# Score and value products of a windowed attention on 64-row tiles, one head each, interleaved in two passes

## The chip, the cores and the metric

One core of a Trainium2 chip. The metric is the device time of one execution in microseconds (us), the median of several runs of the same program. Profiles are of one execution each.

## What is computed

Four sequences of 512 tokens by 128 channels. A cross attention on a short context comes first (it takes the first 50 us and the change touches only where it keeps its operands). Then come six layers, each a windowed attention and a feed-forward block, all in float32. The attention of a layer:

```python
qkv = x @ Wqkv                          # 16 heads of 64
q = l2norm(q) * qs ;  k = l2norm(k) * ksc
q = q*cos*scale + rotate_half(q)*sin*scale      # k with 1/scale
# windows of 32 queries; each sees its own 32 keys and the 32 before
sim  = einsum('bhwie,bhwje->bhwij', bq, bk2) * 8
attn = softmax(where(mask, -max, sim), -1)
out  = einsum('bhwij,bhwje->bhwie', attn, bv2)
x = out @ Wo + x
```

The feed-forward block is a layer norm over channels, `x @ W1`, a gated gelu, `@ W2`, and a residual.

## The kernel before

**Units and slots.** A unit is 128 tokens of one sequence by 8 of the 16 heads of one layer. Eight units make a group (one sequence in one layer, 4 blocks of tokens times 2 halves of the heads), 24 groups make 192 units. Every engine has its own instruction stream, written as a loop over slots n (line 541 for PE, and one each for ACT, DVE, POOL and SP); s is n % 8. In slot n an engine works on several units at different stages; the stages are set by hand, by the order of calls in each loop. Nothing is scheduled by a compiler. Semaphores join the engines.

**A unit's way.** PE makes q and k (`queries_keys`, line 376) and v (`values`, 389). ACT squares q and k (618), DVE sums the squares per head (`sum_squares`, 824), ACT makes a seed of the inverse root, DVE refines it in three short operations (`newton`, 837, 840, 842) and scales k and q into SBUF (`scale_k` 850, `scale_q` 858, which signals `qn_done`). POOL rotates both in six instructions (1053, 1060, 1096 for k, then 1053, 1060, 1089 for q). PE transposes k (410) and q (399), ACT copies them to `kB` (654) and `qT` (645). PE adds the scores (423) to a mask that ACT has put into the bank `sc_bank` (664). DVE takes maxima (865) and subtracts them into `pr` (873), ACT makes the exponentials (671), PE transposes them (`transpose_p`, 436), and the value product (`attend`, 448) multiplies them with the windows of v in `vw`. DVE scales the result into `o` (`scale_o`, 898), PE transposes `o` (461), ACT copies it to `oT` (690), and once per half group PE projects it (472). Slots s = 2, 3, 6 and 7 hold extra long products of PE: the two projections (s = 2, 6), four products of the feed-forward block (s = 3) and its second matrix (s = 7); s = 0, 1, 4, 5 hold one shorter product each. DVE's longest extra work lies in s = 3: two additions to x (907, 908), `rstd_newton` (938, 940), and, after `scale_o`, `layer_norm` (947), for which the four products on PE wait.

**Order in a slot on DVE.** `sum_p`, `newton`, `scale_k`, `scale_q` (of unit n-2), `maxima`, `invert_sum`, `less_maxima` (of n-4), work of the feed-forward block, `sum_squares`, `clamp_squares`, and nearly last `scale_o` (of n-5). PE's first product of a slot waits for `qn_done` of unit n-2:

```python
pe.wait_ge(qn_done, past(u - 1))
```

**Scores and values on PE.** Two heads lie on the 128 partitions of qT. `kB` holds k of both heads in 128 columns with zeros where the other head's rows are (so it is copied by two ACT instructions of 64 partitions), and `vw` is laid out likewise. One product has a contraction of 128, 32 columns of weights (a window of queries) and 128 moving columns (two heads of 64 keys). The array is cut into four column tiles of 32, one per window; 4 pairs of heads times 4 windows make 16 products a unit. Each product in float32 shows as two passes in the profile (x32 a unit).

**PSUM.** q and k have two double banks. One bank is for scores. All else goes round three banks, `RING[i % RINGS]`: each use takes the next turn i, and PE waits until the use three turns earlier has been read (`ring_read`).

**v windows.** ACT copies v from PSUM to `vs` (627). SP then copies its windows to `vw` by DMA (`v_copies`, issues at 1181, 1184, 1187), 8 or 10 transfers a unit, as soon as the value product of two units before is finished. ACT waits before `vs` is used again, six units later.

## Time and profile before

| | us |
|---|---|
| median of 3 runs | 1827.32 |
| lowest, highest run | 1821.96, 1829.11 |
| the profiled execution | 1824.23 |
| its span, first to last instruction | 1822.2 |

| engine | busy us | share of the span |
|---|---|---|
| PE | 1750.3 | 96% |
| DVE | 1619.0 | 89% |
| POOL | 1500.4 | 82% |
| ACT | 1327.5 | 73% |

The profile follows one execution. PE is the matmul part of TensorE, PEld its weight loads, DVE is VectorE, ACT is ScalarE, POOL is GpSimd and SP issues DMAs. In a timeline a row is a run of like instructions: start, length, engine, line of the kernel, output and inputs, and how many; in brackets the engine's idle time before it and what ended that. PE's products overlap, so the length of a row reaches into the next; what a stage costs is the distance from its start to the start of the next. The granted clock of TensorE is at its upper level (1.00) in the whole middle part.

### The profile page before, as it was taken

What the parts mean: (1) busy time and instruction counts of PE and PEld (TensorE: products, weight loads), DVE (VectorE), ACT (ScalarE), POOL (GpSimd) and SP (SyncE); (2) the same over time, 40 slices, a digit from 0 to 9 for tenths busy, and PEclk for the clock granted to TensorE, in tenths of its full rate; (3) what the DMA queues carried; (4) which work ended last, traced back from release to release, by engine and by line L of the source; (5) the groups of instructions that cost most, each with busy time, mean ns of one, the idle gap of its engine ahead of it and who ended that gap; (6) DMA issues with size and microseconds to landing.
All of it is one profiled execution on the core that took longest, in us unless ns stands there. A gap on an engine that the chain in (4) does not pass through costs nothing.

```text
span 1822.2 us, 48666 instructions
## 1 busy us (share of the span) xinstructions
PE 1750.3 (96%) x18122; PEld 1116.2 (61%) x18122; DVE 1619.0 (89%) x2782; ACT 1327.5 (73%) x2362; POOL 1500.4 (82%) x1204
## 2 busy tenths in 40 slices
PE   7699999999999999999999999999999999999986
PEld 6356666666666666666666666666666666666663
DVE  7799998999999989989999999899999998988874
ACT  3577877877778778778777777787776877877763
POOL 4799888888888888988888888888888888888860
PEclk9999999999999999999999999999999999999998
DMA  4132222222222222322223222222222222222221
GB/s 114 28 87 67 68 71 57 60 73 76 71 63 69 63 66 71 76 65 68 63 56 81 72 70 72 54 63 73 75 72 62 68 58 58 59 71 56 56 64 29
DMA packets 155273, 120.59 MB, mean 66 GB/s; under 512 B 42607, under 2 KB 151457, under 8 KB 154913
## 3 DMA queue, kind: packets, MB, share of 16 engines
q1 hardware_dynamic: 155041, 117.48, 25.1%
q8 instruction: 147, 2.41, 0.6%
q14 instruction: 85, 0.70, 0.1%
HBM read 18.79 MB, written 1.05 MB: 11 GB/s over the span
## 4 chain that ended last, share of the span: by engine, by line
PE 77%; DVE 13%; POOL 5%; issue 3%; SPq 1%; ACT 1%; DMA 1%; DVEq 0%; POOLq 0%; ACTq 0%
PE qk_bank L376 17%; PE ring_bank L448 10%; PE ring_bank L472 9%; PE ring_bank L389 8%; PE sc_bank L423 7%; PE ring_bank L516 6%; PE ring_bank L436 4%; PE ring_bank L399 3%; PE ring_bank L527 3%; PE ring_bank L461 3%; PE ring_bank L410 3%; DVE rn L842 2%; DVE step L837 2%; DVE o L898 2%; DVE qkn L858 2%
## 5 line engine op out<-in xcount | busy, mean ns | idle before, releaser
L1053 POOL TENSOR_TENSOR turned<-qkn,tables 128x512 f32<-128x512 f32 x384 | 489.3, 1274 | 209.8 <-DVE qkn L850 201.5
L1060 POOL TENSOR_TENSOR turned<-qkn,tables 128x512 f32<-128x512 f32 x384 | 496.7, 1294 | 0.0
L376 PE MATMUL qk_bank<-wqkv,xT 128*128 128x512 f32 x768 | 366.5, 600 | 18.8 <-DVE qkn L858 18.6
L1089 POOL TENSOR_TENSOR turned<-turned 128x512 f32<-128x512 f32 x192 | 255.0, 1328 | 15.1
L1096 POOL TENSOR_TENSOR turned<-turned 128x512 f32<-128x512 f32 x192 | 245.1, 1277 | 15.1
L448 PEld LDWEIGHTS ring_bank<-vw,pT 128*32 128x32 f32 x6144 | 156.6, 110 | 143.8 <-issue 143.7
L654 ACT ACTIVATE kB<-ring_bank 64x512 f32<-64x512 f32 x384 | 225.3, 587 | 23.5 <-PE ring_bank L410 21.2
L824 DVE TENSOR_REDUCE ss<-sq 128x16 f32<-128x1024 f32 x192 | 232.0, 1208 | 6.8 <-ACT sq L618 6.8
L627 ACT ACTIVATE vs<-ring_bank 128x512 f32<-128x512 f32 x192 | 114.7, 598 | 163.1 <-PE ring_bank L389 153.4
L898 DVE TENSOR_TENSOR o<-ring_bank,rr 128x512 f32<-128x512 f32 x192 | 132.1, 688 | 104.2 <-PE ring_bank L448 101.3
L389 PE MATMUL ring_bank<-wqkv,xT 128*128 128x512 f32 x384 | 216.1, 645 | 1.6 <-DVE x L978 1.6
L664 ACT ACTIVATE sc_bank<-mask_f 128x512 f32<-128x512 f32 x192 | 114.5, 596 | 136.0 <-DVE pr L873 135.6
L448 PE MATMUL ring_bank<-vw,pT 128*32 128x128 f32 x6144 | 208.4, 276 | 0.1
L423 PE MATMUL sc_bank<-kB,qT 128*32 128x128 f32 x6144 | 207.5, 276 | 0.3
L376 PEld LDWEIGHTS qk_bank<-wqkv,xT 128*128 128x128 f32 x768 | 131.2, 191 | 121.7 <-issue 93.4
L618 ACT ACTIVATE sq<-qk_bank 128x1024 f32<-128x1024 f32 x192 | 198.0, 1031 | 0.0
L423 PEld LDWEIGHTS sc_bank<-kB,qT 128*32 128x32 f32 x6144 | 156.0, 109 | 34.7 <-issue 34.7
L472 PE MATMUL ring_bank<-oT,wo 128*128 128x256 f32 x768 | 173.8, 379 | 0.0
L461 PEld LDWEIGHTS ring_bank<-ident,o 128*128 128x128 f32 x768 | 95.5, 141 | 102.1 <-issue 83.9
L472 PEld LDWEIGHTS ring_bank<-oT,wo 128*128 128x128 f32 x768 | 142.2, 190 | 18.1 <-DVE uT L956 0.8
L516 PE MATMUL ring_bank<-xnT,w 128*128 128x512 f32 x288 | 143.3, 609 | 8.5 <-DVE xnT L947 7.3
L850 DVE TENSOR_TENSOR qkn<-qk_bank,rn 128x512 f32<-128x512 f32 x192 | 132.9, 692 | 20.7 <-DVE rn L842 0.9
(169 smaller groups left out, 3129.3 us busy)
## 6 DMA issues: line engine op xcount, KB each, us to landing
vw<-vs SPq DMA_DIRECT2D x1152, 64.0 KB, 2.1
vw<-vs SPq DMA_DIRECT2D x672, 32.0 KB, 1.9
wqkv<-in_L_ffn_Wqkv_dram SPq DMA_DIRECT2D x20, 384.0 KB, 3.5
wo<-in_L_ffn_Wo_dram SPq DMA_DIRECT2D x20, 128.0 KB, 3.3
w<-in_L_ffn_W_dram SPq DMA_DIRECT2D x6, 341.0 KB, 3.4
wqkv<-in_L_ffn_Wqkv_dram SPq DMA_DIRECT2D x1, 1536.0 KB, 9.5
x<-in_x_dram SPq DMA_DIRECT2D x2, 512.0 KB, 4.7
out_dram<-x SPq DMA_DIRECT2D x4, 256.0 KB, 2.3
```

The lines of the kernel that those rows point to most:

```text
L376: mm = pe.matmul(QK[u % 2][:, i * UW:(i + 1) * UW], tok, wqkv[:, layer % 2, cut:cut + UW], start=True, stop=True)
L389: pe.matmul(RING[i % RINGS][:, :], xT[:, b, t * P:(t + 1) * P], wqkv[:, layer % 2, cut:cut + UW], start=True, stop=True).then_inc(ring_mad ...
L423: mm = pe.matmul(heads(SC_BANK[WIN * w:WIN * (w + 1), k * P:(k + 1) * P]), qT[:, u % 2, k, WIN * w:WIN * (w + 1)], kB[:, HP * half + k, :, ...
L448: mm = pe.matmul(heads(RING[i % RINGS][WIN * w:WIN * (w + 1), k * P:(k + 1) * P]), pT[:, u % 2, k, WIN * w:WIN * (w + 1)], vw[:, u % 2, w, ...
L472: mm = pe.matmul(RING[i % RINGS][:, 0:HALF], wo[:, layer % 2, k, :], oT[:, k, HALF * h:HALF * (h + 1)], start=(k == 0), stop=(k == KO - 1))
L516: pe.matmul(RING[i % RINGS][:, :], w1[:, DFF * j + k * P:DFF * j + (k + 1) * P], xnT[:, :], start=True, stop=True).then_inc(ring_made[i % ...
L654: ev = act.activation(kB[64 * h:64 * h + 64, HP * half:HP * half + HP, h, WIN + P * t:WIN + P * t + P], RING[i % RINGS][64 * h:64 * h + 64 ...
L824: dve.tensor_reduce(ss[:, :], heads(sq[:, :]), AX.X, ALU.add).then_inc(ss_done, 1)
L1053: return pool.tensor_tensor(heads(turned[:, u % 2, 2 * i, :]), heads(qkn[:, u % 2, i * UW:(i + 1) * UW]), table.unsqueeze(1).to_broadcast( ...
L1060: return pool.tensor_tensor(halves(turned[:, u % 2, 2 * i + 1, :]), halves(qkn[:, u % 2, i * UW:(i + 1) * UW])[:, :, ::-1, :], table.rearr ...
L1089: pool.tensor_tensor(q, q, turned[:, u % 2, 1, :], ALU.add).then_inc(q_summed, 1)
L1096: pool.tensor_tensor(k, k, turned[:, u % 2, 3, :], ALU.add).then_inc(k_summed, 1)
```

## The change

Each head gets products of its own. A score or value product is now 64 rows (one head), 32 columns of weights and 64 moving columns, and its tile position has a row part too: head 0 of a pair is on rows 0 to 63, head 1 on rows 64 to 127. There are 32 score and 32 value products a unit. `kB` becomes `kT` without the zero blocks (one ACT copy of 128 partitions in place of two), `vw` loses them too, and the memset of `vw` moves from the end of the cross attention to the start.

The products run in two passes, each with both kinds interleaved. Pass one is the score products of head 0 and the value products of head 1; pass two is the rest. Within a pass, the two row halves so write different banks. `scores_values` (pass one) stands behind `values`, `scores_values_rest` (pass two) behind `transpose_o`. A new semaphore, `first_half`, holds pass two until pass one is complete.

```diff
-            def scores(u):
...
+            def score(u, k, w, h):
                 g, layer, b, t, half = place(u)
-                pe.wait_ge(mask_done, u + 1)
-                pe.wait_ge(*evicted("q", u))
+                rows, c0 = slice(DH * h, DH * (h + 1)), P * t + WIN * w
+                return pe.matmul(SC_BANK[WIN * w:WIN * (w + 1), (2 * k + h) * DH:(2 * k + h + 1) * DH],
+                                 qT[rows, u % 2, k, WIN * w:WIN * (w + 1)], kT[rows, HP * half + k, c0:c0 + 2 * WIN],
+                                 start=False, stop=True, tile_position=(DH * h, WIN * w), skip_group_check=True)
+
+            def value(u, k, w, h):
+                rows, bank = slice(DH * h, DH * (h + 1)), RING[turns["pv", u] % RINGS]
+                return pe.matmul(bank[WIN * w:WIN * (w + 1), (2 * k + h) * DH:(2 * k + h + 1) * DH],
+                                 pT[rows, u % 2, k, WIN * w:WIN * (w + 1)], vw[rows, u % 2, w, k * DH:(k + 1) * DH],
+                                 start=True, stop=True, tile_position=(DH * h, WIN * w), skip_group_check=True)
+
+            def scores_values(us, uv):
+                s_on, v_on = 0 <= us < UNITS, 0 <= uv < UNITS
+                if s_on:
+                    pe.wait_ge(mask_done, us + 1)
+                    pe.wait_ge(*evicted("q", us))
+                if v_on:
+                    i = turn("pv", uv)
+                    pe.wait_ge(vw_dma[uv % 2], vw_count(uv))
+                    pe.wait_ge(ring_read[i % RINGS], i // RINGS)
+                    pe.wait_ge(*evicted("p", uv))
                 for k in range(HP):
                     for w in range(NW):
...
+                        if s_on:
+                            last_score = score(us, k, w, 0)
+                        if v_on:
+                            last_value = value(uv, k, w, 1)
...
+            def scores_values_rest(us, uv):
+                s_on, v_on = 0 <= us < UNITS, 0 <= uv < UNITS
+                pe.wait_ge(first_half, past(min(us + 1, UNITS)) + past(min(uv + 1, UNITS)))
...
+                            last_score = score(us, k, w, 1)
+                        if v_on:
+                            last_value = value(uv, k, w, 0)
+                if s_on:
+                    last_score.then_inc(score_mm, 1)
+                if v_on:
+                    last_value.then_inc(ring_made[turns["pv", uv] % RINGS], 1)
...
             for n in range(SLOTS):
                 g, s = n // UPG, n % UPG
                 queries_keys(n)
-                attend(n - 5)
                 values(n)
+                scores_values(n - 3, n - 5)
                 transpose_o(n - 6)
-                scores(n - 3)
+                scores_values_rest(n - 3, n - 5)
                 transpose_p(n - 4)
...
-                for h in range(2):
-                    ev = act.activation(kB[64 * h:64 * h + 64, HP * half:HP * half + HP, h, WIN + P * t:WIN + P * t + P],
-                                        RING[i % RINGS][64 * h:64 * h + 64, :].rearrange("p (k q) -> p k q", q=P), ACT.Copy)
-                ev.then_inc(ring_read[i % RINGS], 1)
+                act.activation(kT[:, HP * half:HP * half + HP, WIN + P * t:WIN + P * t + P],
+                               RING[i % RINGS][:, :].rearrange("p (k q) -> p k q", q=P),
+                               ACT.Copy).then_inc(ring_read[i % RINGS], 1)
...
                 if s == 1:
+                    finish(g - 3)
                     centre(g - 2)
...
-                if s == 1:
-                    finish(g - 3)
...
+            pool.memset(vw[:, :, :, :], 0.0).then_inc(vw_zero, 1)
...
-            pool.wait_ge(b_xT, B)
-            pool.memset(free, 0.0).then_inc(vw_zero, 1)
```

How PE's stream moves, first from the start of a slot with s = 1, before the change (376 q and k, 448 value product, 389 v, 461 transposes of o, 423 scores, 436 transposes of p; the names behind "waits" are semaphores, and `ring_readN` is the reading of bank N):

```order
L376 MATMUL qk_bank<-wqkv,xT 128x512 [waits qn_done]
L376 MATMUL qk_bank<-wqkv,xT 128x512
L448 MATMUL ring_bank<-vw,pT 32x128 [waits ring_read1,ring_read2,vw_dma0]
L448 MATMUL ring_bank<-vw,pT 32x128 x15
L389 MATMUL ring_bank<-wqkv,xT 128x512 [waits ring_read0]
L461 MATMUL ring_bank<-ident,o 128x128 [waits ring_read1]
L461 MATMUL ring_bank<-ident,o 128x128 x3
L423 MATMUL sc_bank<-kB,qT 32x128 [waits ring_read1,mask_done]
L423 MATMUL sc_bank<-kB,qT 32x128 x15
L436 MATMUL ring_bank<-ident,pr 128x128 [waits exp_done,ring_read2]
```

And with the change the same slot's start (373 q and k, 386 v, 414 a score product, 420 a value product; the last two then alternate 16 times):

```order
L373 MATMUL qk_bank<-wqkv,xT 128x512 [waits qn_done]
L373 MATMUL qk_bank<-wqkv,xT 128x512
L386 MATMUL ring_bank<-wqkv,xT 128x512 [waits ring_read2]
L414 MATMUL sc_bank<-kT,qT 32x64 [waits ring_read0,vw_dma0,ring_read1,mask_done]
L420 MATMUL ring_bank<-vw,pT 32x64
```

The value product has gone from second to third place, and its first half shares the first wait with the scores: for the mask, for qT and pT (both `ring_read1`), for its own bank (`ring_read0`), and for the windows of v. In the same slot, the end of pass one, the transposes of o (476) and the start of pass two:

```order
L414 MATMUL sc_bank<-kT,qT 32x64
L420 MATMUL ring_bank<-vw,pT 32x64
L476 MATMUL ring_bank<-ident,o 128x128 [waits ring_read2,ring_read1]
L476 MATMUL ring_bank<-ident,o 128x128 x3
L414 MATMUL sc_bank<-kT,qT 32x64 [waits first_half]
L420 MATMUL ring_bank<-vw,pT 32x64
```

The last value product, which DVE's `scale_o` waits for, lies behind all of these. Last, the same stream from the scores to the transposes of k, before:

```order
L423 MATMUL sc_bank<-kB,qT 32x128 [waits ring_read1,mask_done]
L423 MATMUL sc_bank<-kB,qT 32x128 x15
L436 MATMUL ring_bank<-ident,pr 128x128 [waits exp_done,ring_read2]
L436 MATMUL ring_bank<-ident,pr 128x128 x3
L410 MATMUL ring_bank<-ident,turned 128x128 [waits k_summed,ring_read0]
```

and with the change (466 transposes of p, 407 transposes of k):

```order
L414 MATMUL sc_bank<-kT,qT 32x64
L420 MATMUL ring_bank<-vw,pT 32x64
L466 MATMUL ring_bank<-ident,pr 128x128 [waits exp_done,ring_read2]
L466 MATMUL ring_bank<-ident,pr 128x128 x3
L407 MATMUL ring_bank<-ident,turned 128x128 [waits k_summed,ring_read0]
```

The transposes of k take bank 0 in both. Before, the use of bank 0 three turns earlier was v, which ACT reads; now it is the value product, which DVE reads in `scale_o`.

## Rows read from the trace of the kernel before

**Rows 1.** The page's part 4: shares of the span in the chain.

```profile
PE 77%; DVE 13%; POOL 5%; issue 3%; SPq 1%; ACT 1%; DMA 1%; DVEq 0%; POOLq 0%; ACTq 0%
```

**Rows 2.** Stretches: us, busy (x) of PE, PEld, DVE, ACT, POOL; clock, DMA, GB/s.

```profile
62.00:110.00 48.00, 37.33 (x398) 21.55 (x397) 45.22 (x64) 32.00 (x61) 47.06 (x39) 0.96 0.17 43
...
900.00:972.00 72.00, 70.80 (x757) 44.83 (x750) 66.24 (x111) 54.51 (x98) 61.88 (x50) 1.00 0.26 65
```

**Rows 3.** Timeline of PE: start us, us busy; first q/k product of slots.

```profile
906.03 1.98 PE L376 MATMUL qk_bank<-wqkv,xT 128*128 128x512 f32 x4 [0.43 <-DVE qkn L858]
...
926.74 1.88 PE L376 MATMUL qk_bank<-wqkv,xT 128*128 128x512 f32 x4
...
934.29 1.88 PE L376 MATMUL qk_bank<-wqkv,xT 128*128 128x512 f32 x4
...
942.69 1.98 PE L376 MATMUL qk_bank<-wqkv,xT 128*128 128x512 f32 x4 [0.68 <-DVE qkn L858]
...
952.94 1.88 PE L376 MATMUL qk_bank<-wqkv,xT 128*128 128x512 f32 x4
...
977.86 1.55 PE L376 MATMUL qk_bank<-wqkv,xT 128*128 128x512 f32 x3 [0.36 <-DVE qkn L858]
```

**Rows 4.** Timeline of PE: stages of the slot from 942.69.

```profile
944.61 1.08 PE L448 MATMUL ring_bank<-vw,pT 128*32 128x128 f32 x32
...
945.62 1.13 PE L389 MATMUL ring_bank<-wqkv,xT 128*128 128x512 f32 x2
...
946.58 0.60 PE L461 MATMUL ring_bank<-ident,o 128*128 128x128 f32 x4
...
947.11 1.08 PE L423 MATMUL sc_bank<-kB,qT 128*32 128x128 f32 x32
...
948.61 0.60 PE L410 MATMUL ring_bank<-ident,turned 128*128 128x128 f32 x4
```

**Rows 5.** Timeline of DVE, from `scale_o` to the scaling of q.

```profile
929.80 0.69 DVE L898 TENSOR_TENSOR o<-ring_bank,rr 128x512 f32<-128x512 f32 x1 [0.65 <-PE ring_bank L448]
...
931.00 0.17 DVE L837 SCALAR_TENSOR_TENSOR step<-seed 128x16 f32<-128x16 f32 x1
...
931.20 1.14 DVE L840 TENSOR_TENSOR step<-step,ssm 128x16 f32<-128x16 f32 x1
...
932.38 0.17 DVE L842 SCALAR_TENSOR_TENSOR rn<-step,seed 128x16 f32<-128x16 f32 x1
...
933.26 0.68 DVE L858 TENSOR_TENSOR qkn<-qk_bank,rn 128x512 f32<-128x512 f32 x1
```

**Rows 6.** Timeline of POOL: last of a unit; first and last of the next.

```profile
931.01 1.30 POOL L1089 TENSOR_TENSOR turned<-turned 128x512 f32<-128x512 f32 x1
...
933.49 1.28 POOL L1053 TENSOR_TENSOR turned<-qkn,tables 128x512 f32<-128x512 f32 x1 [1.18 <-DVE qkn L850]
...
939.91 1.30 POOL L1089 TENSOR_TENSOR turned<-turned 128x512 f32<-128x512 f32 x1
```

**Rows 7.** The chain in order of time: start us, us, what.

```profile
916.44 1.72 PE qk_bank L376 x4
```

**Rows 8.** Timeline of ACT: mask, then (third in order) qT.

```profile
944.06 0.60 ACT L664 ACTIVATE sc_bank<-mask_f 128x512 f32<-128x512 f32 x1 [2.01 <-DVE pr L873]
...
945.34 0.60 ACT L645 ACTIVATE qT<-ring_bank 128x512 f32<-128x512 f32 x1
```

**Rows 9.** Timeline of DVE: `scale_o` of s=2, of s=3, and the normalisation.

```profile
909.36 0.68 DVE L898 TENSOR_TENSOR o<-ring_bank,rr 128x512 f32<-128x512 f32 x1
...
920.55 0.69 DVE L898 TENSOR_TENSOR o<-ring_bank,rr 128x512 f32<-128x512 f32 x1
...
921.16 1.05 DVE L947 SCALAR_TENSOR_TENSOR xnT<-dT,cols,rstd 128x512 f32<-128x512 f32 x1
```

**Rows 10.** Timeline of SP: three issues of the v copies.

```profile
910.35 1.87 SPq L1181 DMA_DIRECT2D vw<-vs  x3
```

**Rows 11.** The page's part 6: size and us to landing.

```profile
vw<-vs SPq DMA_DIRECT2D x1152, 64.0 KB, 2.1
```

More of the change, by code:

```diff
@@ L126, in build @@
         rr = sb("rr", [P, 2, HU])
-        free = vw[:, :, :, :, :].rearrange("p k w h n -> p (k w h n)")
-        def take(start, groups, width):
-            return free[:, start:start + groups * width].rearrange("p (a c) -> p a c", c=width)
-        wx_in, wxT = take(0, 4, C), take(512, 4, C)
-        ctx_sb, vx = take(1024, B, C)[0:CTX], take(1536, B, C)[0:CTX]
-        ctxT, kxT = take(2048, B, CTX), take(2560, B, CTX)
+        chunk = lambda c, groups, width: kT[:, c, WIN:WIN + groups * width].rearrange("p (a c) -> p a c", c=width)
+        wx_in, wxT = chunk(0, 4, C), chunk(1, 4, C)
+        ctx_sb, vx = chunk(2, B, C)[0:CTX], chunk(3, B, C)[0:CTX]
+        ctxT, kxT = chunk(4, B, CTX), chunk(5, B, CTX)
         bcol = sb("bcol", [P, 2])
@@ L234, in build @@
         mask_done = sem("mask_done")
+        first_half = sem("first_half")
         score_mm = sem("score_mm")
@@ L436, in transpose_p @@
                     mm = pe.transpose(RING[i % RINGS][:, k * P:(k + 1) * P], pr[:, u % 2, k * P:(k + 1) * P], ident[:, :])
-                mm.then_inc(ring_made[i % RINGS], 1)
-            def attend(u):
-                if not 0 <= u < UNITS:
-                    return
-                i = turn("pv", u)
-                pe.wait_ge(vw_dma[u % 2], vw_count(u))
-                pe.wait_ge(ring_read[i % RINGS], i // RINGS)
-                pe.wait_ge(*evicted("p", u))
-                for k in range(HP):
-                    for w in range(NW):
-                        mm = pe.matmul(heads(RING[i % RINGS][WIN * w:WIN * (w + 1), k * P:(k + 1) * P]),
-                                       pT[:, u % 2, k, WIN * w:WIN * (w + 1)],
-                                       vw[:, u % 2, w, :, k * DH:(k + 1) * DH], start=True, stop=True,
-                                       tile_position=(0, WIN * w))
                 mm.then_inc(ring_made[i % RINGS], 1)
```

34 lines of the change are left out of this document (16 added, 18 removed).

## The prediction

> **What bounds the kernel now.** I read the chain of waits first: three quarters of the span lie on PE and a seventh on DVE, nothing on DMA [rows 1]. The stretch view says how full the engines are: of 72 us in the middle PE is busy for 70.8, DVE for 66.2, POOL for 61.9 [rows 2]. So PE is the bound, but DVE stands only 5 us of 72 behind it. Then the timeline, slot by slot. A **slot** is one turn of the loop over n (one unit of attention, from one first q/k product to the next); eight slots, s = 0 to 7, are one group. The eight slots from 906.03 to 977.86 take 71.8 us [rows 3]: s=2 and s=3 together 20.7, s=4 7.55, s=5 8.4, s=6 10.25, s=7, 0 and 1 together 24.9. Slots 2, 3, 6 and 7 carry the long extra products of PE; the others are the **light** ones, and there PE waits for others.
>
> The loop that decides in a light slot runs through PE and DVE and closes once a slot. PE(n) needs qn_done of unit n-2, which is the last thing that DVE makes in its head of slot n. That stands behind scale_o of the slot before, and scale_o waits for the value product of the slot before. So slot length >= a + b, where **a** is the time from PE's first q/k product to the start of scale_o, and **b** from scale_o's start to PE's next q/k product.
>
> b: scale_o starts at 929.80; the scaling of q that follows it ends at 933.94, and PE starts 0.06 behind such an end (as 942.69 does where it waited): 4.20 us. In it L840 takes 1.14 us where its neighbour L842 takes 0.17; it ends at 932.34, when the POOL instruction of 931.01 ends (932.31) [rows 5, 6]. So a short DVE operation on SBUF is held until the running POOL instruction is over. Without it b is 4.20 - 0.97 = 3.23, say 3.2. The Trainium skill (SBUF — State Buffer, "SBUF: two separate sides") calls the pair of ports of VectorE and GpSimd an exclusive lock; by that rule the trace agrees.
>
> a now: PE 942.69 to 944.61, and the value product ends at 945.69 [rows 3, 4]: 3.0 us, 3.1 with the hand-over. Then a + b is 6.3 to 7.3. DVE has its own work for the first 3.3 us: at 909.36 scale_o starts that long after PE's 906.03 without having waited [rows 3, 9]. At 929.80 it waited 0.65 us [rows 5], so the path is nearly taut already.
>
> **What the change does to PE.** Full array: four passes of 512 columns take 1.72 us [rows 7], so 128 columns take 0.1075. The present score or value stage is 32 passes of 128 columns, 3.44 us one at a time; it takes 1.01 us from its start to the next (944.61 to 945.62) [rows 4]: 0.86 with four tiles side by side, and 0.15 for going in. Each new stage is half of both products: 32 products, 64 passes of 64 columns, again 3.44 us one at a time. With eight tiles (two of rows, four of columns) it is 0.43 + 0.15 = 0.58. Bounds: below that only with more than eight tiles, which there are not; with four at a time still 1.01; and if what spaces the passes is their issue, not the array, the present mean of 1.01/32 = 31.6 ns holds for each of 64: 2.02. I take 0.58, because weight loads and products of one stage now come 32 to a microsecond and the stage comes out at a whole quarter of the array's time, which an issue limit would hit by accident only. Saved on PE: 2 x 0.43 = 0.86 us a slot, 7 us of 72. The number of changes between the two array modes stays four.
>
> **What it does to the loop.** The value product was second in the slot; now it ends with the second pass, behind v, both passes and the transposes of o. And its first pass is queued behind the waits of the scores. Going through a slot in which PE waited at the start:
> - q/k to the next stage is 1.92 now, 1.72 of passes and 0.2 for the first weight load and the change of mode, half each (I split it so; the sum does not hang on it). So v starts at 1.82, takes 0.86, and with the change of mode pass one could issue at 2.78 [rows 4, 7].
> - Its score half waits for qT. ACT copies qT third, behind the mask and the exponentials, and those wait for DVE's pr: the copy ends at 945.34 + 0.60 = 945.94, 3.25 us after PE's start [rows 3, 8]. Now scores start at +4.4 (947.11) and this is hidden; then it is not. Pass one starts at 3.3.
> - 0.58 for it, transposes of o 0.53 (946.58 to 947.11) plus the 0.10 that v takes now, coming after a packed stage (0.96 instead of 0.86), 0.58 for pass two: 5.07. The last product ends 0.07 behind the next start and the hand-over is 0.1 [rows 4]. **a = 5.3**. Where PE did not wait at the start qT is early, and a = 1.72 + 0.96 + 0.58 + 0.63 + 0.58 + 0.17 = 4.7.
>
> DVE's own work still lasts 3.3 us, so it then stands idle for 2 us in each light slot, in order, with the sum, the three Newton steps and both scalings queued behind scale_o, and POOL and PE behind those.
>
> b then: POOL's six instructions of a unit start at 933.49, half a us before the 934.00 at which PE could, and take 7.72 (to 941.21) [rows 5, 6]. So POOL runs until +7.2. The first Newton step comes 1.2 after scale_o, at +6.5, and is held until POOL is through (its last instruction runs from +5.9). From the end of POOL's last instruction to its next first are then 1.18 (printed as its idle time) plus one more short step, 0.2. **Light slot: 7.72 + 1.18 + 0.2 = 9.1 us**, for any a from 4.7 to 6.0; beyond, a + 3.2.
>
> The eight slots:
> - s=2 and 3: scale_o of s=2 at 5.3; from there to the scale_o of s=3 DVE works 11.2 us (its other work of both slots lies there, so it does not shrink) (909.36 to 920.55), to the end of the normalisation 1.66 (922.21), and from there PE, whose gate products need it, takes 4.5 to the next slot (926.74) [rows 3, 9]: 22.7 instead of 20.7.
> - s=4: DVE ahead, a = 4.7, b between 3.2 and 4.2: 8.4 (7.55 now). s=5: 9.1 (8.4).
> - s=6: passes end at 5.1, then the transposes of p; those of k wait for scale_o to read their bank (order rows above), 5.3 + 0.69 + 0.06 = 6.05, and from there to the next slot as now 948.61 to 952.94, 4.3 [rows 3, 4]: 10.4 (10.25). What PE saves is eaten by qT and that bank.
> - s=7: PE bound, no wait at the start: transposes of k at 4.7 + 0.75 = 5.45, those of k and q 0.44 each (four passes of 128 columns), the second matrix six passes of 0.43: 8.9. s=0 and 1: 9.1 each. 27.1 together (24.9).
>
> Sum 77.7 against 71.8: +5.9, times 22 groups = +130. In the opening, without feed-forward work, POOL is the bound (busy 47.1 of 48 us [rows 2]) at 7.7 a slot; the 11 slots from the first value product (n = 5) to the end of group 1 go to 9.1: +15. In the tail the products thin out: 0.
>
> **At nothing:** the one copy of kT in place of two saves ACT 0.6 us, hidden by ACT's 2.01 us wait for DVE [rows 8]. The v copies on SP start as now when the value product of two units before is done; nine or ten issues of 0.62 and 2.1 to land [rows 10, 11] make 8.4, well inside two slots of 9.1; ACT's copy of v, which waits for them, comes at about +4.6 and its bank is wanted at +5.1. Cover gone, each 0.5 late would cost up to 0.5 a slot. Smaller memsets at the start lie before POOL's first work. `finish` moves over nothing but DVE's last group.
>
> The profiled execution took 1824.2 us (span 1822.2), 3 below the median of the runs. 1824 + 130 + 15 = 1969; I say **1970**.
>
> **Rivals.**
> 1. *Row tiles do not run side by side* (the change does not do what it says): passes 1.01. a = 6.2, light 9.4; 23.6 + 9.3 + 9.4 + 11.3 + 9.8 + 18.8 = 82.2, +10.4 x 22 + 18: 2070. Nothing in the trace has two row tiles, so nothing speaks against it.
> 2. *Issue bound*: passes 2.02, a = 8.2, light 11.4; 25.6 + 11.3 + 11.4 + 13.3 + 11.8 + 22.8 = 96.2, +24.4 x 22 + 42: 2400. For it: the number of passes doubles, 31.6 ns is all that the rows show.
> 3. *Faster*: PE's saving decides and the late value product does not, because DVE's work still fills the time before scale_o. The group then falls to what DVE is busy, 66.2 [rows 2]: -5.6 x 22: 1700. For it: PE is the bound and is relieved by more than that. It decides if a stays below about 3.5, where DVE's own work covers it; against it: PE's passes alone add up to 4.7.
> 4. *No change*: the loop is there, but qT is in time (a = 4.7) and POOL holds nothing (b = 3.22): light 7.9, 22.1 + 7.9 + 7.9 + 9.6 + 8.8 + 15.8 = 72.1, +0.3 x 22: 1831. Against it: POOL is at work for 62 of 72 us [rows 2], so a free moment of 0.6 us must fall just right.
>
> The Trainium skill (TensorE: Matmul & The Clock Gate, Part 1, "Wait — 56ns, not 53.3ns?") says that starts of matmuls never come closer than about 25 ns however few the columns. By it a pass would be 64 x 25 ns = 1.6 us, an estimate from the page, and the kernel about 2260. No row here parts that from rival 2; the 31.6 ns lie above it, so the trace neither bears it out nor contradicts it.
>
> **How the numbers follow.** Forecast 0.68, rival 1 0.13, rival 2 0.06, rival 3 0.07, rival 4 0.06. The range, 1850 to 2085, holds the forecast with a light slot from 8.3 to 9.5 and rival 1; outside are the other three, 0.19. Faster by over 0.5% (what a measurement of this kernel can tell; its runs lie within 0.4%): rival 3 and a tail, 0.08. Same: most of rival 4, 0.05. Slower: 0.87.
>
> **What would show it.** Right: PE's two pass stages near 0.6 us each; DVE's idle time before scale_o, waiting for the value product, at some 2 us in nearly each slot (now 0.65 at 929.80); light slots at 9 us; PE busy near 85%; POOL waiting for the k scaling in almost each slot, and the first Newton step ending with POOL's last instruction. Wrong: stages of 1.0 or 2.0 (rivals 1, 2), or scale_o not waiting (3), or Newton steps of 0.2 in light slots (4).

## The result and the profile after

| | before | after |
|---|---|---|
| median | 1826.4 us (1822.0 to 1829.1, 4 runs) | 2075.4 us (2066.2 to 2086.0, 4 runs) |
| ratio, 95% interval | | 1.137 (1.131 to 1.143) |
| span of the profiled execution | 1822.2 us | 2083.9 us |

The kernel became 13.7% slower, 105 us more than forecast and 10 us inside the upper end of the range. The page of the kernel after, its parts 1, 3 and 4, and the queue's line of before:

```profile
span 2083.9 us, 73056 instructions
...
PE 1789.4 (86%) x30410; PEld 1117.8 (54%) x30410; DVE 1464.9 (70%) x2782; ACT 1196.3 (57%) x2170; POOL 1490.3 (72%) x1203
...
q8 instruction: 243, 3.98, 0.8%
...
PE 56%; DVE 28%; issue 10%; SPq 3%; POOL 1%; DMA 1%; DVEq 1%; ACT 1%; POOLq 0%; ACTq 0%
```

```profile
q8 instruction: 147, 2.41, 0.6%
```

DVE's part of the chain rose from 13% to 28% [rows 1]. "Issue", time in which an engine waited for nothing that the profile shows, rose from 3% to 10%; the order alone does that too, since experiment 1 below, which has no stop, shows 9%. The groups of instructions of the kernel after (line, engine, operation, shapes, count | busy us, mean ns | idle time before, and what ended it):

```profile
L1064 POOL TENSOR_TENSOR turned<-qkn,tables 128x512 f32<-128x512 f32 x384 | 487.9, 1270 | 470.8 <-DVE qkn L864 470.8
...
L912 DVE TENSOR_TENSOR o<-ring_bank,rr 128x512 f32<-128x512 f32 x192 | 132.8, 691 | 509.8 <-PE ring_bank L420 509.4
L373 PE MATMUL qk_bank<-wqkv,xT 128*128 128x512 f32 x768 | 382.9, 622 | 62.6 <-DVE qkn L872 62.6
...
L414 PE MATMUL sc_bank<-kT,qT 64*32 64x64 f32 x12288 | 332.9, 224 | 74.2 <-issue 58.0
L420 PE MATMUL ring_bank<-vw,pT 64*32 64x64 f32 x12288 | 337.8, 225 | 26.5 <-issue 26.5
```

and `scale_o` of the kernel before:

```profile
L898 DVE TENSOR_TENSOR o<-ring_bank,rr 128x512 f32<-128x512 f32 x192 | 132.1, 688 | 104.2 <-PE ring_bank L448 101.3 <-ACT qT L645 0.5
```

DVE's wait for the value product grew from 101 to 509 us, 2.7 us a slot: this is the late value product of the forecast. The 84 us of "issue" in the two lines of the passes nobody had forecast; the same two groups of before, L423 and L448, have 0.3 and 0.1 us of idle time.

A **light slot** after (993.29 to 1002.37, s = 5), DVE and then POOL, and PE's next q/k product:

```profile
998.83 0.69 DVE L912 TENSOR_TENSOR o<-ring_bank,rr 128x512 f32<-128x512 f32 x1 [2.17 <-PE ring_bank L420]
999.44 0.68 DVE L894 TENSOR_REDUCE rs<-pr 128x8 f32<-128x512 f32 x1
1000.03 0.47 DVE L851 SCALAR_TENSOR_TENSOR step<-seed 128x16 f32<-128x16 f32 x1
1000.53 0.18 DVE L854 TENSOR_TENSOR step<-step,ssm 128x16 f32<-128x16 f32 x1
1000.75 0.17 DVE L856 SCALAR_TENSOR_TENSOR rn<-step,seed 128x16 f32<-128x16 f32 x1
1001.02 0.69 DVE L864 TENSOR_TENSOR qkn<-qk_bank,rn 128x512 f32<-128x512 f32 x1
1001.63 0.68 DVE L872 TENSOR_TENSOR qkn<-qk_bank,rn 128x512 f32<-128x512 f32 x1
```
```profile
999.19 1.27 POOL L1100 TENSOR_TENSOR turned<-turned 128x512 f32<-128x512 f32 x1
1001.86 1.26 POOL L1064 TENSOR_TENSOR turned<-qkn,tables 128x512 f32<-128x512 f32 x1 [1.39 <-DVE qkn L864]
```
```profile
1002.37 1.98 PE L373 MATMUL qk_bank<-wqkv,xT 128*128 128x512 f32 x4 [0.84 <-DVE qkn L872]
```

`scale_o` waits 2.17 us (2 forecast) and starts 5.54 us into the slot (a, 5.3 forecast). The first Newton step takes 0.47 instead of 0.17: it ends at 1000.50, when POOL's instruction of 999.19 is over (1000.46). The slot is 9.08 us (9.1 forecast).

**The passes.** A pass here is one half of the products: 32 products, which show as 64 matmul records, and 64 weight loads. The timeline of PE in the slot from 985.00 (the first two starts of pass one, the transposes of o, the start of pass two and the transposes of p):

```profile
987.67 0.24 PE L414 MATMUL sc_bank<-kT,qT 64*32 64x64 f32 x1
987.68 0.24 PE L420 MATMUL ring_bank<-vw,pT 64*32 64x64 f32 x1
...
988.46 0.66 PE L476 MATMUL ring_bank<-ident,o 128*128 128x128 f32 x4
989.04 0.24 PE L414 MATMUL sc_bank<-kT,qT 64*32 64x64 f32 x1
...
989.83 0.66 PE L466 MATMUL ring_bank<-ident,pr 128*128 128x128 f32 x4
```

A pass takes 0.79 us from its start to the next stage (987.67 to 988.46), not 0.58. **A stop in pass two** of the slot from 1002.37:

```profile
1007.43 0.22 PE L414 MATMUL sc_bank<-kT,qT 64*32 64x64 f32 x1
1009.29 0.21 PE L420 MATMUL ring_bank<-vw,pT 64*32 64x64 f32 x1 [1.65 <-issue]
```

The pass stands still for 1.86 us, six of its 64 matmul records short of its end; DVE's `scale_o`, and all behind it, come that much later. There are 41 such gaps of over 0.9 us between the starts of neighbouring products of a pass, 72.2 us together, and none in the kernel before. (The expectations below speak of 47 stops in this kernel; this count gives 41.) All 41 stand at the same place in the count of TensorE's records, waits for semaphores included: at number 194 or 195 modulo 256. What the DMA queues did in two stretches around this stop:

```profile
q8 instruction: 1, 0.02, 42.1%
```
```profile
DMA packets 0, 0.00 MB, mean 0 GB/s; under 512 B 0, under 2 KB 0, under 8 KB 0
```

The first is 1006.4 to 1006.6: one packet of 16384 bytes, from 1006.49 to 1007.84. The second is 1007.9 to 1009.2: nothing moves, and PE goes on at 1009.29. There are as many of these packets (243) as times that the count passes 194 modulo 256, and so it is in kernels with other counts (147 packets for 37705 records before, 195 for 49993 in experiment 3): one packet belongs to 256 records, 64 bytes to each. In each of the 41 stops PE goes on 1.2 to 1.7 us after such a packet has landed (median 1.4). So the suspicion was: **PE has used up its instructions and waits for the next 256.** The passes with the transposes of o between them are 264 instructions in 2.0 us; they are called the **burst** below.

The slots, in us, as medians over the slots of the same s behind group 1 (from the starts of the q/k products, the last group left out; the mean of a group stands apart, since most of what the stops cost is only in it):

| s | 0 | 1 | 2 | 3 | 4 | 5 | 6 | 7 | sum | mean group |
|---|---|---|---|---|---|---|---|---|---|---|
| before | 7.56 | 8.08 | 10.25 | 10.45 | 7.55 | 8.21 | 10.25 | 9.27 | 71.6 | 71.9 |
| after | 8.86 | 9.06 | 10.72 | 11.11 | 8.30 | 9.06 | 10.63 | 9.93 | 77.7 | 82.1 |

The sum of the medians is the 77.7 of the forecast; the mean lies 4.4 us above. Kernels without a stop have a difference too, of 0.3 us (before) and 0.5 us (experiment 1), and the slots after without a stop have means that sum to 78.0, so some 4 us of a group are the stops'. Over the profiled execution the 261.7 us between the two spans are: first slot 5.4 later; groups 0 and 1 +21.7; the other 22 groups +224.6; behind the last q/k product +10.0.

### The profile page after: what moved, and what is told of

The parts are those of the page before. It is cut to its first block, busy times and chain, and to the rows that moved or that the text cites. A ratio compares the mean times of both kernels' runs of the same rounds, so it can differ in the third digit from the quotient of the medians.

```text
span 2083.9 us, 73056 instructions
## 1 busy us (share of the span) xinstructions
PE 1789.4 (86%) x30410; PEld 1117.8 (54%) x30410; DVE 1464.9 (70%) x2782; ACT 1196.3 (57%) x2170; POOL 1490.3 (72%) x1203
## 3 DMA queue, kind: packets, MB, share of 16 engines
q1 hardware_dynamic: 155041, 117.48, 21.8%
HBM read 18.79 MB, written 1.05 MB: 10 GB/s over the span
## 4 chain that ended last, share of the span: by engine, by line
PE 56%; DVE 28%; issue 10%; SPq 3%; POOL 1%; DMA 1%; DVEq 1%; ACT 1%; POOLq 0%; ACTq 0%
PE qk_bank L373 13%; PE sc_bank L414 9%; PE ring_bank L386 6%; PE ring_bank L420 6%; DVE o L912 6%; PE ring_bank L487 5%; PE ring_bank L476 5%; PE ring_bank L531 5%; DVE qkn L872 4%; DVE rs L894 3%; DVE ss L838 2%; PE ring_bank L407 2%; PE ring_bank L396 2%; SPq L1192 1%; DVE pr L887 1%
## 5 line engine op out<-in xcount | busy, mean ns | idle before, releaser
L373 PE MATMUL qk_bank<-wqkv,xT 128*128 128x512 f32 x768 | 382.9, 622 | 62.6 <-DVE qkn L872 62.6
L414 PEld LDWEIGHTS sc_bank<-kT,qT 64*32 64x32 f32 x12288 | 267.6, 106 | 247.1 <-issue 246.1
L414 PE MATMUL sc_bank<-kT,qT 64*32 64x64 f32 x12288 | 332.9, 224 | 74.2 <-issue 58.0
L420 PE MATMUL ring_bank<-vw,pT 64*32 64x64 f32 x12288 | 337.8, 225 | 26.5 <-issue 26.5
L420 PEld LDWEIGHTS ring_bank<-vw,pT 64*32 64x32 f32 x12288 | 258.6, 106 | 43.9 <-issue 43.7
L386 PE MATMUL ring_bank<-wqkv,xT 128*128 128x512 f32 x384 | 200.2, 603 | 0.1
L487 PE MATMUL ring_bank<-oT,wo 128*128 128x256 f32 x768 | 183.6, 394 | 0.4 <-DVE o L912 0.4
L407 PE MATMUL ring_bank<-ident,turned 128*128 128x128 f32 x768 | 130.2, 295 | 37.5 <-DVE o L912 36.4
L668 ACT ACTIVATE kT<-ring_bank 128x512 f32<-128x512 f32 x192 | 115.3, 600 | 75.7 <-PE ring_bank L407 75.3
L694 ACT ACTIVATE pT<-ring_bank 128x512 f32<-128x512 f32 x192 | 116.5, 607 | 73.0 <-PE ring_bank L466 73.0
```

The costliest lines, as they stand in the source:

```text
L373: mm = pe.matmul(QK[u % 2][:, i * UW:(i + 1) * UW], tok, wqkv[:, layer % 2, cut:cut + UW], start=True, stop=True)
L386: pe.matmul(RING[i % RINGS][:, :], xT[:, b, t * P:(t + 1) * P], wqkv[:, layer % 2, cut:cut + UW], start=True, stop=True).then_inc(ring_mad ...
L414: return pe.matmul(SC_BANK[WIN * w:WIN * (w + 1), (2 * k + h) * DH:(2 * k + h + 1) * DH], qT[rows, u % 2, k, WIN * w:WIN * (w + 1)], kT[ro ...
L420: return pe.matmul(bank[WIN * w:WIN * (w + 1), (2 * k + h) * DH:(2 * k + h + 1) * DH], pT[rows, u % 2, k, WIN * w:WIN * (w + 1)], vw[rows, ...
L487: mm = pe.matmul(RING[i % RINGS][:, 0:HALF], wo[:, layer % 2, k, :], oT[:, k, HALF * h:HALF * (h + 1)], start=(k == 0), stop=(k == KO - 1))
```

## The experiments

Two theories. **A**: the place of the value product sets the slot (a + b with POOL's hold), and on top of it the stops are waits for instructions. **B**: small products cost by their number, or something else stops PE. Each run was compared with runs of the kernel before on the same chip; their ratio is given with its 95% interval.

**1. The order without the tiles.** The 128-row products of before, in the change's order (in this diff and the next ones only PE's loop or the line that matters is shown; experiments 1 and 2 and the second kernel of 7 also move DVE's `finish(g - 3)` forward in s = 1, as the change does):

```diff
-                attend(n - 5)
                 values(n)
+                scores_values(n - 3, n - 5)      # k = 0, 1: score, value, score, value ...
                 transpose_o(n - 6)
-                scores(n - 3)
+                products(n - 3, n - 5, (2, 3))   # k = 2, 3
```

> The kernel before, with its 128-row products, kB and padded vw, issued in the order of the change: q and k, v, scores and values of k = 0 and 1 interleaved, transposes of o, scores and values of k = 2 and 3, transposes of p. Theory A (what the forecast rests on: the value product ends late, so o is scaled late, and with it the keys and queries of the next slot): a light slot becomes 9.1 to 9.7 us, a group of 8 slots about 79, the time 1950 to 2080, and no stops near the end of the products. Theory B (small products and their number are what the change pays for): a light slot stays at 7.6 to 8.2 and the time at 1820 to 1850.

Measured: 2097.6 us, ratio 1.147 (1.145 to 1.150), 18 us above the top of A's range. The order alone makes the kernel slower than the whole change (1.137, 1.131 to 1.143). Its light slot (DVE, then PE):

```profile
995.73 0.69 DVE L908 TENSOR_TENSOR o<-ring_bank,rr 128x512 f32<-128x512 f32 x1 [2.95 <-PE ring_bank L424]
996.34 0.68 DVE L890 TENSOR_REDUCE rs<-pr 128x8 f32<-128x512 f32 x1
996.93 0.17 DVE L847 SCALAR_TENSOR_TENSOR step<-seed 128x16 f32<-128x16 f32 x1
```
```profile
989.43 1.98 PE L376 MATMUL qk_bank<-wqkv,xT 128*128 128x512 f32 x4 [0.53 <-DVE qkn L868]
...
998.97 0.70 PE L376 MATMUL qk_bank<-wqkv,xT 128*128 128x512 f32 x1 [0.53 <-DVE qkn L868]
```

a is 6.30 and b 3.24: so late that POOL is through, the Newton step takes 0.17, and b is the 3.2 of the forecast. No stop (147 packets of instructions, as before). The mean group is 82.55, medians 82.05, not the 79 expected.

**2. The value product behind v**, and `finish` as said.

```diff
-                attend(n - 5)
                 values(n)
+                attend(n - 5)
```

> The kernel before with one thing moved: its undivided value product behind the v projection instead of ahead of it, everything else in place. Theory A (DVE's wait for the value product closes a loop with VectorE, GpSimd and the transposes): o is ready 0.6 us later in each slot than before, of which the slack of the loop takes a part: light slots 8.0 to 8.6 and a time of 1840 to 1890. Theory B (the order of the two does not matter, TensorE is busy with one or the other): 1822 to 1832, and the wait of VectorE for the value product grows without a longer slot.

Measured: 1864.1 us, 1.020 (1.018 to 1.023), the time of A. DVE's wait for the value product rises from 101 to 178 us. The slots are not all as A says. `scale_o` starts 0.9 us later in the light slots (a = 3.92), and yet s = 0 and s = 4 stay at 7.51; s = 5 goes from 8.21 to 8.34 and s = 1, where `finish` has moved too, from 8.08 to 8.53. Most of the 1.3 us of a group is in s = 3 (10.45 to 11.48), where the products of the feed-forward block wait for what DVE does behind `scale_o` (their wait for it rises from 7.3 to 24.3 us in all):

```profile
L898 DVE TENSOR_TENSOR o<-ring_bank,rr 128x512 f32<-128x512 f32 x192 | 132.8, 692 | 179.0 <-PE ring_bank L448 178.3
```

**3. 64-row tiles in the place where the products were**, for the scores alone:

```diff
                 attend(n - 5)
                 values(n)
+                scores(n - 3, 0)      # kT, 64 rows, h = 0
                 transpose_o(n - 6)
-                scores(n - 3)
+                scores(n - 3, 1)      # h = 1, behind first_half
```

> The kernel before with the score product alone per head on 64-row tiles: kT in place of kB (one key copy an ACT instruction in place of two), a pass for h = 0, the transposes of o, a pass for h = 1 behind the wait for the first pass; the value product stays as it was, undivided on 128 rows and ahead of the v projection. Theory A (the place of the value product is what costs, 64-row tiles by themselves do not): the light slot stays at 7.5 to 8.2 us, time 1805 to 1845, few or no stops, since 128 + 16 instructions stand between two waits and not 272. Theory B (64-row products cost by their number and by the wait between the passes): light slots of 8.5 and more, 1880 to 1980.

Measured: 1857.8 us, 1.016 (1.012 to 1.019), between the two ranges and no stops. `scale_o` stays at 3.06. The light slots stay as a whole: s = 0 and 4 go from 7.55 to 7.86 and s = 1 and 5 from 8.1 and 8.2 to 7.9, as A says; the four heavy ones take 0.2 to 0.3 us more each. A pass with one row group is 32 matmul records in 0.59 us (987.04 to 987.63), 14 ns from start to start in it; two of them 1.18 against 1.01 of the undivided product, and one more change of mode. So 64-row tiles save nothing by themselves here: in the runs in which both row groups take turns the spacing is 10 ns.

**4. Filling the count of instructions.** Does the count decide the stops? First with empty instructions ahead of q/k, in chosen slots:

```diff
+                for _ in range(PADS[n] if n < UNITS else 0):
+                    pe.nop(nofuse=True)
                 queries_keys(n)
```

> The change with empty instructions (1838 in all, in 39 of the 192 slots, 44 to 67 at a time) on TensorE's stream ahead of the q-k projection, so that the two passes with the transposes of o between them (264 instructions in 2.0 us) never start in the 60 positions of the 256-instruction count from which the trace of the change shows a stop of 1.3 to 3.8 us near their end. Theory A (the stops are waits for the stream's next 256 instructions, which the count alone sets): 0 to 3 of the 47 stops are left, the groups of 8 slots fall from a mean of 82.0 us to about 78, and the time falls by 75 to 105 us, to 1970 to 2000. Theory B (something else stops the engine every fourth slot, as a buffer or a DMA would): the number of stops stays near 47 and the time stays at 2075 or rises by up to 20 for the added instructions.

> The control of the run before: nearly as many empty instructions (2042 in all), placed so that the passes do start inside those positions, in 57 slots instead of 48. Theory A: 50 to 60 stops of 1.3 to 3.8 us, and a time of 2075 to 2110. Theory B: no difference between this run and the other with empty instructions, by more than 0.5%.

Measured: 2077.1 and 2076.6 us. Neither theory was tested: the built programs hold no such instruction (62288 TensorE records and 243 packets of instructions in both, as in the change). They only show how well a time repeats, and what varies in it: 43 and 39 stops. Then with a real instruction:

```diff
-                    pe.nop(nofuse=True)
+                    pe.ldweights(ident[0:32, 0:16].bitcast(BF16))
```

> The two runs with empty instructions turned out to hold none: their TensorE stream has the same 62288 records and the same 243 fetches of 16 KB as the change, so they were two more runs of the change itself. Here the filler is a weight load of 32 x 32 bf16 values that nothing uses, 1838 in all, at the same places: ahead of the q-k projection in the slots whose passes would start in the bad 60 of 256 positions. Theory A (the stops are waits for the next 256 instructions, set by the count alone): 0 to 5 of the 47 stops are left, and the time falls by 60 to 100 us, to 1975 to 2015 (the fillers take about 10 ns each, most of it beside a wait). Theory B (something else stops the engine): near 47 stops, 2075 to 2095.

> The control: 2042 of the same unused weight loads, placed so that the passes start inside the bad positions in 57 slots. Theory A: 50 to 60 stops, 2075 to 2115. Theory B: within 0.5% of the run before it.

Measured: 2081.1 us, 1.139 (1.136 to 1.142), and 2137.9 us, 1.171 (1.166 to 1.176). The control did as A says: 58 stops, 107.8 us, all at 194 or 195 modulo 256 although the fillers moved the passes to other places in the count. The first run missed A's range with 37 stops, 64.5 us, and lies in B's (2075 to 2095): my table stood one slot early, so that passes were moved into the bad positions (those from which the change shows a stop). Corrected, with more fillers:

> The first run with fillers had put them one slot early, so that many passes came to start inside the bad positions after all (37 stops, 14 of them at one such position), and it showed a second thing: in the slots behind a long row of TensorE's extra products (s = 0, 3, 6, 7) the passes also stop when the boundary lies up to 88 positions ahead of them. Here 3510 unused weight loads (18 ns each in that run, 63 us in all) stand in the right slots and keep every burst clear of both. Theory A (the stops are waits for the next 256 instructions): 0 to 5 stops are left of 41, their 72 us and the time at half clock behind them come back, less the part of the 63 us of fillers that no wait hides: 2005 to 2060, and a mean clock of 0.98 or more. Theory B (the stops come from something else): 35 or more stops, 2090 or more.

Measured: 2047.1 us, 1.122 (1.119 to 1.124), mean clock 0.974, the time of A. 7 stops are left in the passes, 13.9 us. The lines of the products in the control, and in the corrected run:

```profile
L446 PE MATMUL ring_bank<-vw,pT 64*32 64x64 f32 x12288 | 341.5, 225 | 76.0 <-issue 76.0
```
```profile
L446 PE MATMUL ring_bank<-vw,pT 64*32 64x64 f32 x12288 | 329.4, 225 | 0.0
L440 PE MATMUL sc_bank<-kT,qT 64*32 64x64 f32 x12288 | 326.0, 224 | 43.2 <-issue 30.9 <-DVE xT L950 5.6 <-DVE xT L1011 5.4
```

Instructions that compute nothing made the kernel 28 us faster than the change, in spite of their own 63 us (3510 x 18 ns; the expectation of the first filler run had 10 ns each), and badly placed ones 63 us slower. The clock and the number of stops missed A's figures a little. In part the waits have only moved: PE and its weight loads also wait for "issue" at stages that are not passes, 28.5 us at the transposes of p (L492), 4.9 there in the change.

**5. An earlier qT.**

```diff
-                copy_qT(n - 3)       # head of the slot
                 norm_seed(n - 1)
@@
+                copy_qT(n - 2)
                 fill_mask(n - 2)
```

> The change with ScalarE's copy of qT moved from the head of a slot to the slot before, ahead of the mask: in the six of eight slots in which pass one now starts 3.11 us into the slot, behind that copy, it should start at 2.67 as in the others, and VectorE's scaling of o at about 5.1 instead of 5.5 us. Theory A (in the light slots GpSimd's queue still holds the next keys and queries, so that the slot follows the scaling of o by half or less): 0.1 to 0.25 us less in each of the six slots, 15 to 35 us in all, time 2040 to 2060. Theory B (the slot is the scaling's start plus 3.2 us everywhere): 0.44 us less in each of them, about 60 us in all, 2015 or less. Both leave the stops, near 40 to 48 of them.

Measured: 2062.8 us, 1.129 (1.124 to 1.135), 3 us above the top of A's range and far from B's. `scale_o` comes at 5.17 instead of 5.49 in s = 5, and the slot stays 9.06 to the hundredth; s = 6 gains 0.33 (10.30), s = 7 loses 0.30 (10.23), and the medians sum to 77.6, as in the change. So the slots gave back next to nothing, less than A expected; what is less is the stops, 36 of 57.6 us against 41 of 72.2, and that no run ties to qT.

**6. The same, with v between the passes.**

```diff
-                values(n)
                 scores_values(n - 3, n - 5)
+                values(n)
                 transpose_o(n - 6)
                 scores_values_rest(n - 3, n - 5)
```

> The run before with the v projection moved between the passes: q and k, pass one, v, transposes of o, pass two. The passes with what stands between them then hold 276 instructions in about 3.1 us instead of 268 in 2.0, while pass two still ends about 5.2 us into the slot. Theory A (a stop is the time by which the 256 instructions are used up sooner than the next ones can be fetched): stops get shorter by about 1.1 us each, to 0 to 0.9 us, near 40 of them or fewer, their sum from 72 to under 30 us, and the time falls to 1985 to 2030. Theory B (the stop is a fixed cost, paid at the boundary whatever the pace): still 40 stops of 1.3 us and more, and a time within 1% of the run before it.

Measured: 2009.9 us, 1.102 (1.099 to 1.105), 53 us less than the run before it. 8 stops are left, 9.6 us:

```profile
L420 PE MATMUL ring_bank<-vw,pT 64*32 64x64 f32 x12288 | 330.9, 225 | 1.9 <-issue 1.8
L414 PE MATMUL sc_bank<-kT,qT 64*32 64x64 f32 x12288 | 327.1, 224 | 18.4 <-ACT sc_bank L678 8.1 <-issue 7.6
```

This is A. As many instructions, as many packets (243), the value product as late (a = 5.33), but 2.9 us for the burst instead of 2.0: the stops go. Their place does not explain it. In the run before, the count passes 194 modulo 256 behind the first 192 records of a burst in 59 slots, and 34 of these have a stop; here in 62 slots, and 7 have one. This is the clearest of the runs on the stops. (One thing else changes: the transposes of p now need the bank of the value product, and wait 170 us for `scale_o` in all. It costs, so it does not explain the gain in time; whether a pause behind the burst helps against the next stop no run tells.)

**7. Both passes ahead of v, with 64-row and with 128-row products.**

```diff
                 queries_keys(n)
-                values(n)
-                scores_values(n - 3, n - 5)
                 transpose_o(n - 6)
+                scores_values(n - 3, n - 5)
                 scores_values_rest(n - 3, n - 5)
+                values(n)
```

(qT as in 5, and ACT copies oT ahead of v.) The second kernel has the products of experiment 1 in this order.

> The change with both passes ahead of the v projection: q and k, transposes of o, pass one, pass two, v, transposes of p; the copy of qT is moved one slot up, ahead of the mask, so that only the mask (1.98 us into the slot) holds pass one. Theory A (the place of the value product sets the slot): its end falls from about 5.3 us into the slot to about 3.9, light slots become 7.6 to 8.3 us, the heavy ones lose the time of TensorE that 64-row tiles save, and the time without the stops would be about 1750 to 1830; with 40 to 60 stops of 1.3 to 2 us left in it, 1820 to 1930. Theory B (64-row passes or their number cost by themselves, not by their place): 2000 or more.

> The order of the run with both passes ahead of v (q and k, transposes of o, products, v, transposes of p, qT copied one slot earlier), with the 128-row products, kB and padded vw of the kernel before. Theory A (64-row tiles save some 0.3 us of TensorE a slot and their stops cost more than that): no stops, slots 0.2 to 0.4 us longer than there where it did not stop (a group of 77 to 78.5 us against medians of 75.2 and a mean of 78.7), time 1930 to 1985, so a little faster than its 2006. Theory B (the 64-row tiles are worth their stops): slower than it, 2020 or more.

Measured: 2005.7 us, 1.098 (1.093 to 1.102), with 46 stops of 88.0 us; and 1946.2 us, 1.066 (1.063 to 1.068), without a stop. The first missed A's range by 76 us and is at the edge of B's (2000 or more). Its light slots are 7.8 to 8.6, two of them above A's 8.3, and the heavy ones are not shorter than before (s = 2 and 3: 11.3 and 10.7). So the place of the value product is not all: the stops, which come with the number of small products, cost as B has it. The second is in A's range. In the same order the larger products are 60 us faster: the 64-row tiles save TensorE 1.95 - 1.73 = 0.22 us a slot there and lose it, and more, in the stops.

`scale_o` against slot, medians in us, of all orders that were run:

| | before | late v | 128-row, ahead of v | 64-row, ahead of v | earlier qT | v between | the change | 128-row, its order |
|---|---|---|---|---|---|---|---|---|
| a, s = 5 | 3.06 | 3.92 | 4.44 | 4.21 | 5.17 | 5.33 | 5.49 | 6.31 |
| slot, s = 5 | 8.21 | 8.34 | 8.78 | 8.55 | 9.06 | 9.05 | 9.06 | 9.54 |
| slot, s = 4 | 7.55 | 7.51 | 8.01 | 7.81 | 8.30 | 8.35 | 8.30 | 9.35 |
| mean group | 71.9 | 73.2 | 76.5 | 78.7 | 81.0 | 79.1 | 82.1 | 82.6 |

Every order with a later value product is slower than the kernel before, the least by 2.0%. A version that beats it was not found, and the numbers don't point to one: what TensorE could save is 0.44 us in a slot that it bounds.

## Why the prediction was right, and what it missed

**The loop (right).** a = 5.3 and 4.7 forecast, 5.49 (s = 5) and 5.07 (s = 4) measured. Two misses cancel in part in the first: the passes take 0.42 us more than their term, and pass one starts at 3.1 (qT), not at 3.3. In s = 4, where qT is early, pass one starts at 2.67 as forecast (2.68) and only the passes' miss is left. The plateau of 9.1 for a from 4.7 to 6.0 is in the table: 5.17, 5.33 and 5.49 all give 9.05 to 9.06, and at 6.31 the slot is a + 3.23, as "beyond, a + 3.2" had it. The Newton step held until POOL's instruction ends is there at a = 5.54 (0.47 us) and gone at 6.30 (0.17). Experiment 2, a move of 0.9 us, shows little of the loop itself: the light slots hardly answer, and its cost comes through DVE's work in s = 3. The loop is seen in the kernels with a of 4.2 and more. That the *order* is the cause, and not the tile, experiment 1 shows: order alone +10.4 us a group (71.6 to 82.05), the tiles -4.4 (to 77.7), the stops and what follows them +4.4 (to 82.1). The last two cancel by chance. The moved `finish` was not run alone; with the value product behind v it is in experiment 2, so it costs 1.3 us a group at most if the other move gains nothing.

**The slots (right in sum).** s = 5, 0 and 1: 9.1 forecast, 9.06, 8.86, 9.06. s = 4: 8.4, 8.30 measured. s = 6: 10.4, 10.63. s = 2 and 3: 22.7 forecast, 21.8. s = 7: 8.9 forecast, 9.93; it was taken as bound by PE, and it was 9.27 before. Its miss and the one of s = 2 and 3 cancel.

**The pass (mis-sized).** "With eight tiles it is 0.43 + 0.15 = 0.58": 0.79. The row tiles do run side by side, since the 64 matmul records of a pass take less than the 1.01 of rival 1, but the reason for leaving out an issue limit did not hold. The 31.6 ns of that limit (rival 2) had the time for going in with them; the starts of before were 26 ns apart. In rows of the pass the first starts are 7 ns apart (987.67, 987.68, ...) and later ones 16 ns apart in pairs: the mean is 10 ns, where 64 x 10 = 0.64 and 0.15 for going in make 0.79. PE saves 0.44 us a slot, not 0.86. The rule that was weighed there, of the Trainium skill (TensorE: Matmul & The Clock Gate, Part 1, "Wait — 56ns, not 53.3ns?"), that starts never come closer than about 25 ns, does not hold for these tiles; the trace differs by its 7 ns, and the measurement decides.

**Rival 1 as a check.** Its sum for passes of 1.01 us was 82.2 us a group with light slots of 9.4. Experiment 1 is that case (1.05 us a pass, without a row tile): 82.05, and 9.35 and 9.54. The working of the slots held to 0.2%, though its time, 2070, is 28 us below the 2097.6 of that run.

**The missing term.** The forecast had no price for 264 TensorE instructions in 2 us. The profiled execution took 262 us more than before where the forecast had 145, so it is 117 us short there (105 by the medians). Of these, 95 lie in the 22 groups, 7 in the first two, 5 in the start and 10 in the tail. The 95 are the term that was missing: 4.4 us a group x 22 = 97, most of them the stops. The cost is more than the stop: the 41 stops are 72 us. Between the control and the first filler run 43 us more of stops went with 57 us more of time (71 between the two profiled executions, in which the stops were counted), with 204 more fillers, 4 us. A part of the rest is the clock, below. The diff shows the instructions beforehand: each product of 128 rows became two, so the TensorE instructions of a slot went up by 128, in one place.

**Opening, start and tail.** The first two groups took 21.7 us more, 15 forecast, and 20.6 in experiment 1, which has no stop: the excess is the order's. The first slot started at 56.7 instead of 51.3 us, but experiment 4's first run, with the same instructions, has 51.3: the start differs between executions. The tail took 10 us more, 0 forecast; experiment 1 has 11 and experiment 2 nothing, so an order as late as the change's costs there too, where the forecast had nothing.

**Luck in the number.** 2075 lies in the range, but the upper end, 2085, had been set for rival 1 and not for stops, and experiment 1, which is rival 1's case, took 2097.6, beyond it. The range held the result because the tiles gave back about what the stops took.

## What to carry to other kernels

Before splitting products to fill a systolic array better, ask who waits for the *last* of them: here a saving of 0.4 us on the busiest engine was paid for with 2.4 us of lateness for an engine that closes the loop. Count instructions as well as columns: where a burst uses up an engine's instructions faster than they come in, the stop appears in no semaphore and no queue of the program, only as "issue", at a fixed remainder of the instruction count. If the same engine has other work that is not urgent (here the v projection), put it into the burst; that took 53 us off here, though not enough to reach the kernel before.

## What the runs showed of the hardware

**Instructions are fetched 256 at a time, and PE can outrun the fetch.** One packet of 16384 bytes on its own queue goes with each crossing of 194 modulo 256, at the median 1.1 us behind it (one at the start of the kernel is ahead of it), and takes 0.9 to 1.6 us. PE never went past the next crossing sooner than 1.1 us after that packet had landed, in none of the 14 profiled executions, and in the stops it went past 1.1 to 1.7 us after. In the stop shown, the crossing before is at 1004.51, its packet lands at 1007.84, and PE passes the next crossing at 1009.29. In the kernels with 128-row products the shortest such distance is 3.5 us. So a stop needs two things: that the 256 instructions between two crossings go fast, which holds when most of them are the burst (of 109 crossings in the first 160 records of a burst none has a stop, of 59 behind its first 192 records 40 have one), and a packet that comes late. At the stops the packet had started 4.4 us after its crossing at the median, and in some slots it started up to 9 us after (crossing 602.38, packet at 611.15, with a row of large products in between). What holds it back stays open.

**Behind a stop the clock often falls.** Stretches of the kernel after (us, busy of PE, PEld, DVE, ACT, POOL; granted clock; DMA; GB/s), with a stop at 965.3 to 966.8:

```profile
960.00:963.00 3.00, 2.84 (x6) 1.06 (x6) 3.00 (x6) 1.47 (x3) 2.92 (x3) 1.00 0.29 73
963.00:966.50 3.50, 2.21 (x130) 1.81 (x130) 0.49 (x2) 2.69 (x6) 3.42 (x4) 1.00 0.15 40
966.80:970.20 3.40, 3.06 (x13) 2.48 (x14) 2.76 (x7) 1.62 (x3) 0.72 (x2) 0.68 0.14 37
970.20:973.60 3.40, 3.40 (x14) 2.87 (x13) 3.37 (x6) 2.50 (x5) 3.32 (x3) 0.82 0.26 67
973.60:977.00 3.40, 3.40 (x44) 1.67 (x43) 3.32 (x5) 2.40 (x5) 3.32 (x4) 1.00 0.67 178
```

The granted clock goes from 2.4 to 1.2 GHz for part of the two stretches behind the stop. A stretch at the lower level begins within 8 us of 20 of the 41 stops; 11 others are not behind a stop. From 100 us to the end the kernel after has 130 us at the lower level, the kernel before 17, experiment 1 without stops 36, experiment 6 33, and the control with 58 stops 190.

**Small products.** 64-row, 32-column products start 7 ns apart at best and 10 on the mean with eight tiles in turn, 14 with four (experiment 3); 128-row ones with four tiles 26. An unused weight load of 32 x 32 takes 18 ns.
